# Layer norm's eps: from an addition on GpSimd to a bias in ScalarE's squares, in a state-space block with an FP4 feed-forward

## What is computed

```python
u = silu(conv3(x, conv_w))                      # three taps along the sequence
B, C = split(u @ W_bc + b_bc)                   # 16 states each
dt = softplus((u @ W_dt + b_dt) @ W_dtp + b_dtp)
h[t] = exp(A * dt[t]) * h[t-1] + B[t] * x[t] * dt[t]      # scan along the sequence
y = sum_n(C * h) + x * Dcoeff
x1 = layernorm(x + y)                           # first norm
g, v = fp4(x1) @ fp4(w_gate).T, fp4(x1) @ fp4(w_up).T
out = layernorm(x1 + fp4(silu(g) * v) @ fp4(w_down).T)    # second norm

def layernorm(x, eps=1e-05):
    m = mean(x); v = var(x)
    return (x - m) / sqrt(v + eps)
```

## Time and profile before

| | us |
|---|---|
| timed runs | 383.5, 389.12, 389.15 (median 389.12) |
| the profiled execution, its own time | 383.09 |
| its span, first to last instruction | 381.3 |
| around the span | 1.8 |
| mean granted TensorE clock, as a share of full speed | 0.898 |
| instructions | 3999 |
| ACT, groups of four squares (L549) | 16 |
| POOL, additions of eps (L708) and powers (L710) | 16 and 16 |

### The profile page before, as it was taken

The page is one execution under the profiler, slowest core; times in us unless marked ns, Lnnn a source line. Parts: engine busy times, 40 slices in busy tenths (PEclk is TensorE's granted clock), DMA queues, the critical chain, the costliest instruction groups (busy, mean ns, idle before and its releaser), DMA issues.

```text
span 381.3 us, 3999 instructions
## 1 busy us (share of the span) xinstructions
PE 266.0 (70%) x1130; PEld 122.8 (32%) x1130; DVE 319.7 (84%) x364; ACT 228.2 (60%) x505; POOL 289.7 (76%) x171
## 2 busy tenths in 40 slices
PE   2457659678856879688868786878687664772683
PEld 1123122223311335233613261336222432261372
DVE  4875979999999998989899998899889997356670
ACT  3453755955596459755995488657964664053234
POOL 0092655687588999899889998998899899955542
PEclk9859898799989999799999998899969895897798
DMA  3740460190028002720192009200730001000001
GB/s 63 159 117 1 92 157 2 31 203 14 2 58 192 1 0 59 163 55 2 22 200 55 2 0 202 74 2 2 172 75 2 0 0 28 0 3 0 28 2 55
DMA packets 19246, 21.86 MB, mean 57 GB/s; under 512 B 6096, under 2 KB 15128, under 8 KB 19224
## 3 DMA queue, kind: packets, MB, share of 16 engines
q1 hardware_dynamic: 18504, 21.05, 24.4%
q10 hardware_dynamic: 720, 0.56, 0.8%
HBM read 2.72 MB, written 2.10 MB: 13 GB/s over the span
## 4 chain that ended last, share of the span: by engine, by line
PE 31%; ACT 19%; DVE 17%; POOL 13%; issue 12%; SPq 3%; DMA 2%; ACTq 1%; POOLq 0%; DVEq 0%
PE ps_prep L1216 7%; DVE states L957 7%; PE ps_b L1223 5%; DVE db L941 4%; POOL product L700 3%; ACT c_rep L541 3%; SPq L422 3%; ACT ps_decay L465 3%; PE ps_y L1182 3%; PE ps_prep L1203 3%; POOL qh_norm L721 2%; POOL qh_norm L716 2%; PE ps_f L1248 2%; POOL hq L759 2%; DMA dt_rep<-dtx 2%
## 5 line engine op out<-in xcount | busy, mean ns | idle before, releaser
L700 POOL TENSOR_TENSOR product<-states,c_rep 128x1024 f32<-128x1024 f32 x64 | 151.0, 2364 | 30.6 <-DVE states L957 28.8
L465 ACT ACTIVATE ps_decay<-dt_rep,aneg 128x512 f32<-128x512 f32 x128 | 87.4, 692 | 39.6 <-DVE states L957 36.5
L941 DVE SCALAR_TENSOR_TENSOR db<-ps_b,bbc_rep,dt_rep 128x2048 f32<-128x2048 f32 x31 | 72.5, 2338 | 10.7 <-PE ps_b L1223 8.3
L957 DVE TENSOR_TENSOR_SCAN states<-ps_decay,states,db 128x512 f32<-128x512 f32 x64 | 78.9, 1259 | 2.4 <-POOL product L700 2.4
L957 DVE TENSOR_TENSOR_SCAN states<-ps_decay,db 128x512 f32<-128x512 f32 x64 | 75.4, 1203 | 0.4 <-ACT ps_decay L465 0.2
L1216 PE MATMUL ps_prep<-u_feat,wbc_rep 128*128 128x512 f32 x56 | 37.1, 749 | 21.0 <-ACT c_rep L541 20.8
L1223 PE MATMUL ps_b<-u_feat,wbc_rep 128*128 128x512 f32 x64 | 40.5, 719 | 15.5 <-DVE db L941 15.4
L1248 PE MATMUL ps_f<-gate_t,xq_t 128*128 128x352 f32 x64 | 30.1, 554 | 13.7 <-DVE hidden L1012 8.1
L1182 PE MATMUL ps_y<-product,gather 128*32 128x512 f32 x256 | 37.1, 654 | 2.9 <-POOL product L700 2.9
L579 ACT ACTIVATE gate_tanh<-ps_f 128x352 f32<-128x352 f32 x32 | 14.8, 464 | 37.6 <-PE ps_f L1248 37.6
L541 ACT ACTIVATE c_rep<-ps_prep,bbc_rep 128x512 f32<-128x512 f32 x28 | 19.4, 693 | 16.6 <-PE ps_prep L1216 16.0
(11 more groups left out here) (172 smaller groups left out, 502.9 us busy)
## 6 DMA issues: line engine op xcount, KB each, us to landing
dt_rep<-dtx SPq DMA_DIRECT2D x124, 128.0 KB, 2.4
x_tok<-in_L_attn_x SPq DMA_DIRECT2D x8, 256.0 KB, 3.1
out<-y_out SPq DMA_DIRECT2D x8, 256.0 KB, 2.4
dt_rep<-dtx ACTq DMA_DIRECT2D x4, 128.0 KB, 3.7
hidden<-in_L_ffn_w_down SPq DMA_DIRECT2D x1, 176.0 KB, 3.4
x_feat<-in_L_attn_x SPq DMA_DIRECT2D x8, 0.5 KB, 2.7
hidden<-in_L_ffn_w_gate SPq DMA_DIRECT2D x1, 128.0 KB, 2.7
hidden<-in_L_ffn_w_up SPq DMA_DIRECT2D x1, 128.0 KB, 2.6
```

The lines of the kernel that those rows point to most:

```text
L465: nc.scalar.activation(ps_decay[BANK_OF[k]][:], dt_rep[p][:, c, 0, :], ACT.Exp, scale=aneg[:, c, m:m + 1]).then_inc(decay_done, 1)
L700: nc.gpsimd.tensor_tensor(product[:, j % PRODUCTS], states[p][:, first:first + 2, :], over(c_rep[p][:, j // SET_PAIRS, :], 2), ALU.mult).t ...
L941: nc.vector.scalar_tensor_tensor(out=db[m % DB][:], in0=over(ps_b[:], QUADS), scalar=bbc_rep[:, 0, m:m + 1], in1=dt_rep[p][:, :, 1, :], op ...
L957: nc.vector.tensor_tensor_scan(out=states[p][:, k % ring, :], data0=ps_decay[BANK_OF[k]][:], data1=db[k // QUADS % DB][:, k % QUADS, :], i ...
```

## The change

eps leaves POOL. ACT's square gets a bias, sqrt(eps / 128), for which a column `root_eps` with one value for each partition is set at the start. The sum of (x/sqrt(128) + sqrt(eps/128))^2 over 128 elements is the mean of the squares plus eps plus a term with the sum of x, which is 0 for rows of mean 0. `norm` becomes the power alone; the buffer var_eps and the semaphore between addition and power go. ACT waits for the constants once, at its start.

```diff
-        eps = sb("eps", [128, TILES])
+        root_eps = sb("root_eps", [128, 1])
...
+            act.wait_ge(masks, 4)
             act.wait_ge(setup_order, 1)
             nc.scalar.activation(table_in[:, 0:1], x_feat[0][:, 0:1], ACT.Exp)
...
                 for i in range(TILES):
                     last = nc.scalar.activation(squares[n][:, i], tile(i), ACT.Square, scale=D ** -0.5,
-                                                accum_out=norm_bufs[n][0][:, i:i + 1])
+                                                bias=root_eps[:], accum_out=norm_bufs[n][0][:, i:i + 1])
                 last.then_inc(var_done[n], 1)
...
-            nc.gpsimd.memset(eps[:], EPS).then_inc(masks, 1)
+            nc.gpsimd.memset(root_eps[:], (EPS / D) ** 0.5).then_inc(masks, 1)
             pool.wait_ge(masks, 4)
-            orders = [Order(pool, norm_order[n], POOL_NORM) for n in range(2)]
...
             def norm(u, n):
 
-                var, var_eps, rstd = norm_bufs[n]
+                var, rstd = norm_bufs[n]
                 pool.wait_ge(var_done[n], u.at(1, 1))
-                orders[n].unit(u)
-                orders[n].mark(nc.gpsimd.tensor_tensor(var_eps[:], var[:], eps[:], ALU.add))
-                orders[n].need()
-                nc.gpsimd.tensor_tensor(rstd[:], var_eps[:], power[:], ALU.pow).then_inc(rstd_done[n], 1)
+                nc.gpsimd.tensor_tensor(rstd[:], var[:], power[:], ALU.pow).then_inc(rstd_done[n], 1)
```

More of the change, by code:

```diff
@@ L91 @@
 DVE_GATE, DVE_QUANT = 2, 2
-POOL_NORM, POOL_CODES = 1, 2
+POOL_CODES = 2
 PREP_MM, PREP_EVAC = 3 + SETS, 1 + SETS
@@ L229, in build @@
         r_feat = sb("r_feat", [128, UNIT])
-        norm_bufs = [(sb(f"var{n}", [128, TILES]), sb(f"var_eps{n}", [128, TILES]), sb(f"rstd{n}", [128, TILES]))
-                     for n in range(2)]
+        norm_bufs = [(sb(f"var{n}", [128, TILES]), sb(f"rstd{n}", [128, TILES])) for n in range(2)]
         x1 = [sb(f"x1_{h}", [128, TILES, D]) for h in range(X1)]
@@ L333, in build @@
         var_done = [sem(f"var_done{n}") for n in range(2)]
-        norm_order = [sem(f"norm_order{n}") for n in range(2)]
         rstd_done = [sem(f"rstd_done{n}") for n in range(2)]
@@ L568, in gate @@
                         last = nc.scalar.activation(x1[f.first % X1][:, i, :], r_tile(i), ACT.Copy,
-                                                    scale=norm_bufs[0][2][:, i:i + 1])
+                                                    scale=norm_bufs[0][1][:, i:i + 1])
                     last.then_inc(x1_done, 1)
@@ L612, in normalised @@
                     last = nc.scalar.activation(
-                        y_out[o][:, i * D:(i + 1) * D], tile(i), ACT.Copy, scale=norm_bufs[1][2][:, i:i + 1])
+                        y_out[o][:, i * D:(i + 1) * D], tile(i), ACT.Copy, scale=norm_bufs[1][1][:, i:i + 1])
                 last.then_inc(y_done, 1)
```

## The result

The changed kernel takes 390.1 us (median of 22 runs, 386.07 to 394.95); the kernel before, run beside it, 385.86 (22 runs, 383.5 to 391.53). The ratio is 1.0114 with a 95% interval of 1.0087 to 1.014: slower by 1.1%, some 4.4 us, and within the 2% that I forecast. I had forecast 391.6 and 0.6%. The three runs shown ahead of the prediction lay high; with 19 more the median of before came down by 3.3 us. Every ratio here is taken over the fast runs alone, those within 1.5% of the fastest of the same kernel, while the medians are over all runs; in the rounds of the experiments about half of before's runs fall out of the ratio by that (13 of 28, 14 of 23, 13 of 25), so a ratio and the two medians beside it can differ by a per cent.

The account below looks back on a forecast made before the run. No engine alone was taken as the bound; the chain goes round between them. Steps +1.8 +0.7 and tail +1.1 -1.1 gave +2.5 us on the 389.12 median: 391.6 us, range 390.0 to 393.1, with rivals 383.0 to 394.0.

Parts of the forecast that it names:

- POOL's additions, 0 in the steps: Steps: dropping POOL's additions only lengthens its idle times, so 0 us reaches the end.
- The tail's 0.8 us: Tail: without the addition, the power drawn out beside DVE is done 0.8 us earlier, bounds 0 and 1.7.
- the middle case: Tail: the power's writing waits for the second DVE instruction, so it is done about 0.8 us earlier.
- the upper bound: Tail: the power gets through between the two DVE instructions and is done 1.7 us earlier.
- The strict reading: Tail: the power is held while either DVE instruction runs; gain 0 there, 0.3 us in place of 1.1.
- 1.1 for ACT less 1.1 for POOL: Tail: three groups of squares cost 1.1 us; the earlier power (0.8) and last norm (0.27) save 1.1.
- The price of the column, 0.09 us a square and 0.36 a group: ACT's squares: the bias column adds 0.09 us to each square's pitch, 0.36 us per group of four.
- rival 3: ACT's squares: a column square does not overlap its accumulator reading; +12.3 us, 401.4 us; chance 0.05.
- First norm whole, second by half: Steps: five first-norm groups count fully, 1.8 us; four second-norm groups by half, 0.7 us.
- The first (the column hidden in the pitch): ACT's squares: the column costs nothing in the pitch and the tail gives its most; -2.0 us, 387.1 us; chance 0.13.
- The second (the delay doesn't reach the end in the steps): Steps: the squares' delay is there but does not reach the end; 0 us, 389.1 us; chance 0.12.
- The fourth, about the level of the median: Whole kernel: mechanism as forecast, but the median falls at the lowest earlier run; 386.0 us; chance 0.15.

Follow-up runs that it names:

- POOL's half alone: Changed kernel without the bias column, so no addition on POOL and eps left out: 383.27 us, ratio 0.9978 to the kernel before.
- ACT's half alone: Kernel before with the bias column in ACT's squares; POOL's addition stays and adds 0: 391.76 us, ratio 1.0201 to the kernel before.
- With the clock held: Changed kernel, column in one norm only, two useless multiplications in TensorE's wait for c_rep: ratio to before 0.9971 (first norm), 0.9948 (second).
- the number and the filling: Changed kernel with the bias as a number, plus two useless multiplications in TensorE's wait for c_rep: 381.79 us, ratio 0.998 to before.
- the filling: Changed kernel plus two useless 512-column multiplications on TensorE behind the first one for C, in its wait for c_rep: 386.85 us, ratio 1.0053 to before.
- the first norm alone: Changed kernel with the bias column in the first norm's squares only, the second norm leaving eps out: 388.42 us, ratio 1.0131 to before.

## Why the prediction was right, and where it was not

**POOL's additions, 0 in the steps: right.** POOL's half alone leaves the sum of the steps at 158.75 against 158.77, and with the bias as a number, which has the same POOL half, it is 157.61. So nothing that goes beyond the 1 us by which two such profiles differ.

**The tail's 0.8 us: the place right, the size wrong twice.** At the power itself I took the middle case, and it was the upper bound, 1.65 us against my 1.7. The power does get in between the two DVE instructions and doesn't wait for the second. The strict reading of the Trainium skill's rule (GPSIMD Engine Reference, section 1, Specifications), that GpSimd contends with DVE instructions that have two SBUF inputs, would have made the gain 0; it doesn't hold here, since the power ends 0.8 us before the second instruction does. The gate multiplication, which I expected to be late next, takes little of the gain: ACT's gate_tanh starts 4.77 us behind xq's start, where it was 6.32, or 1.55 less. Further on most of it is lost. To the last power, 0.57 us is left of my 1.1 at the same granted clock (28.72 us from xq on before, 28.15 with the bias as a number), and 0.43 between ACT's half alone and the whole change (29.18 and 28.75). The tail as a whole, where I had 1.1 for ACT less 1.1 for POOL, took 1.5 us more: ACT's half alone lost 1.7 there. How much of this is the clock's isn't shown.

**The price of the column, 0.09 us a square and 0.36 a group: right.** Measured 0.088 in the square's length, and in the group 1.39 less 1.01 = 0.38. By the Trainium skill's 93 ns for each pointer operand (ScalarE: Activation LUTs, What ACT_TABLE_LOAD costs) it is 0.37 too, and the runs with one and two columns agree with its "each". A square that isn't overlapped (rival 3) did not occur.

**First norm whole, second by half: wrong in the split, near in the sum.** With the clock held, the first norm's group costs 0.35 us a step, which is the 0.36 that I took for each, and the second's costs nothing in the steps, where I had 0.7. DVE's unbroken row of work fits that: DVE is busy for all of the 10 us. Reading the chain alone misled me. It names the second group in all four steps, in the one at full clock (at 193.22) too, and it still does in the profile where the column in the second norm costs the steps nothing:

```profile
197.55 1.26 ACT hq_t L549 x7
```

So a group can stand in the chain and still have room. The delay reaches c_rep and is gone behind it: from c_rep of this step to the next step's first square it is 24.95 us, where it is 25.32 with the number and the filling.

**What the sum lacked: the clock.** The sum has no term for it. I took TensorE's durations as given. The profile before had the answer in its page, in the row of the granted clock, and in the groups (L1216 at a mean of 749 ns, where its shortest takes 592). In the two profiles the four steps lost 5.1 us; the first norm's time explains 4 x 0.35 = 1.4, and the other 3.7 I put down to the clock. For 2.0 of them that is tested. With the filling the column costs the steps only 160.58 less 157.49 = 3.1, so 2.0 of the 5.1 are gone with it; of the 3.1 that stay, 1.4 are again the first norm's time, and 1.7 lie in the one step of 41.25, behind the wait for hq, where the clock is seen to fall; no run with the column holds it there. This fits that half the change costs about as much as the whole, and that the changed kernel's loss is 1.8 times my 2.5 by the ratio (4.4 of 386).

**Rivals 1, 2 and 4.** The first (the column hidden in the pitch) is out by the timelines. The second (the delay doesn't reach the end in the steps) holds for the second norm and not for the first. The fourth, about the level of the median, came true in part: before's median was 385.86 with more runs, so the time came out 1.5 us under my number although the loss was larger. The point was close by luck, because two errors of mine had opposite signs.

Open: why the first norm alone also pulls the clock down in the stretch of C. It lengthens an earlier wait of TensorE for hq_t, from 1.28 to 1.65 us, and leaves the one ahead of C at 2.11; no run filled the earlier wait alone. So it is shown that holding the clock in the stretch of C gives back 2.0 us of the loss there, and not shown what makes it fall: a wait that grows by 0.36 us is one reading, a shift in time against the moments when the clock changes is another, and no run tells them apart.

## What to carry to other kernels

Before an operand becomes a column in memory, see whether a number in the instruction would do: the same bias as a number cost ScalarE nothing, as a column 0.09 us on every instruction. Taking work from an engine that waits ahead of it for another one gives it back as waiting, whatever its busy share. A group that stands in the chain may still have room, so its price on the path is a question for an experiment. And where TensorE waits in a chain of small dependent steps, look at the granted clock in that stretch first: in one pair of profiles 0.36 us more on ACT in one group of each step went with some 1.2 us a step (163.63 less 158.77, over four), and a kernel's durations are not constants under a change of timing.

## What the runs showed of the hardware that I had not expected

TensorE's clock was at half, 1.2 GHz, behind a wait of 2.46 us in which it did nothing, and at 2.4 GHz through all four stretches when two useless multiplications of 512 columns stood in that wait; pairs for C took 2.08 and 1.13 us. Behind waits of 2.10 and 2.11 us it was at half in some steps and full in others. A power on POOL with 4 elements beside DVE instructions with two SBUF inputs took 2.38 us in place of 1.02, but ended 0.86 us behind the first of them and 0.8 ahead of the second's end. In the start, the program stood up to 5 us later in one profile than in another, between kernels that don't differ there, and the clock rose later in it: the first power is at 68.13 us where the clock was 0.97 from 25 to 30 us, and at 73.47 where it was 0.50 there and 0.52 from 30 to 35.
